# Attention and mixture of experts on one core: rank products in fp32r, a third turn of 64 columns, and the router's weights turned first

## The reference

```python
x = L0_attn_x
xn = _layernorm(x, axis=-1)
# attention: y = xn @ U (32 columns); softmax(-|y_i - y_j|^2) over the block's tokens, times xn
# feed-forward on xn (2048 tokens):
logits = rms_norm(xf) @ router_w.T                    # 8 experts
topk_p, topk_i = jax.lax.top_k(softmax(logits), 2)
order = jnp.argsort(~sel, axis=1, stable=True)        # sel: which tokens chose expert e
dispatch = order[:, :capacity]                        # capacity 320: the first 320 of them
xg = xf[dispatch]
eout = einsum(silu(xg @ rg) * (xg @ ru), rd)          # per expert: 128 -> 512 -> 128
routed = zeros.at[dispatch].add(eout * weight)
shared = silu(xn @ sg) * (xn @ su) @ sd               # 128 -> 1024 -> 128
return x + attention + shared + routed
```

## Time and profile before

| what | value |
|---|---|
| median of 3 runs | 158.22 us (157.16 to 158.99) |
| span of the profiled execution | 156.0 us |
| what lies outside the span, by the fastest, the median and the slowest run | 1.16, 2.22 and 2.99 us |
| PE busy | 151.1 us (97%) |
| DVE, ACT, POOL busy | 117.5, 103.8, 83.3 us |

### The profile page before, as it was taken

The page is one execution under the profiler, slowest core; times in us unless marked ns, Lnnn a source line. Parts: engine busy times, 40 slices in busy tenths (PEclk is TensorE's granted clock), DMA queues, the critical chain, the costliest instruction groups (busy, mean ns, idle before and its releaser), DMA issues.

```text
span 156.0 us, 3115 instructions
## 1 busy us (share of the span) xinstructions
PE 151.1 (97%) x964; PEld 135.6 (87%) x964; DVE 117.5 (75%) x290; ACT 103.8 (67%) x217; POOL 83.3 (53%) x102
## 2 busy tenths in 40 slices
PE   6899999999999999999999999999999999999992
PEld 6878878798999988888878999999999999878992
DVE  3799969899824599999997676786787786545962
ACT  3258999999479398768756669899686566343200
POOL 7562531357777778878400004698988857454000
PEclk9999999999999999999999999999999999999999
DMA  4999999992111117536059400314232111118477
GB/s 118 278 274 119 147 277 335 345 335 77 57 53 51 51 32 220 158 80 191 0 119 299 136 0 2 149 39 119 60 105 70 32 46 34 29 29 263 100 267 217
DMA packets 26640, 20.72 MB, mean 133 GB/s; under 512 B 2334, under 2 KB 22841, under 8 KB 26625
## 3 DMA queue, kind: packets, MB, share of 16 engines
q1 hardware_dynamic: 24832, 17.89, 44.3%
q0 software_dynamic: 1792, 2.65, 5.6%
HBM read 12.36 MB, written 7.92 MB: 130 GB/s over the span
## 4 chain that ended last, share of the span: by engine, by line
PE 92%; DMA 2%; ACT 2%; DVE 2%; POOL 1%; issue 1%; SPq 0%
PE bank L1257 9%; PE bank L1342 9%; PE bank L1177 8%; PE bank L1179 8%; PE bank L1178 8%; PE bank L1282 8%; PE bank L1288 8%; PE bank L1285 8%; PE bank L1398 5%; PE bank L1400 5%; PE bank L1399 5%; PE bank L1414 2%; PE bank L1242 2%; DMA acc<-in_L_attn_x_dram 2%; PE bank L1425 2%; PE bank L1197 1%
## 5 line engine op out<-in xcount | busy, mean ns | idle before, releaser
L676 ACT ACTIVATE silu<-bank 128x512 f32<-128x512 f32 (+1 forms) x64 | 33.3, 520 | 29.3 <-PE bank L1288 29.1
L570 POOL DMA_INDIRECT slots_dram<-row,slot_i x32 | 34.0, 1063 | 10.9 <-issue 9.4
L1008 DVE TENSOR_TENSOR bank<-bank,silu 128x320 f32<-128x320 f32 (+1 forms) x48 | 27.1, 565 | 15.6 <-ACT silu L676 12.6
L589 POOL DMA_INDIRECT routed_dram<-eo,xg x24 | 23.0, 957 | 11.5 <-DVE eo L1048 6.3
L1014 DVE TENSOR_TENSOR hid_lo<-bank,hid_hi 128x320 fp32r<-128x320 f32 (+1 forms) x48 | 26.2, 546 | 0.0
L684 ACT CAST hid_hi<-bank 128x320 fp32r<-128x320 f32 (+1 forms) x48 | 22.9, 477 | 0.0
L577 POOL TENSOR_TENSOR ew_lo<-sw_raw,ew_hi 128x1024 fp32r<-128x1024 f32 x3 | 7.2, 2416 | 19.4 <-ACT ew_hi L700 19.4
L1342 PEld LDWEIGHTS bank<-sd,hid_s 128*128 128x128 f32 x128 | 14.8, 192 | 0.3
L1008 DVE TENSOR_TENSOR hid_s<-bank,silu 128x512 f32<-128x512 f32 x16 | 11.0, 685 | 5.5 <-PE bank L1179 5.2
L1257 PEld LDWEIGHTS bank<-row,probs 128*128 128x128 f32 x128 | 14.8, 192 | 0.2
L1342 PE MATMUL bank<-sd,hid_s 128*128 128x128 f32 x128 | 15.0, 275 | 0.0
(11 more groups left out here) (204 smaller groups left out, 363.8 us busy)
## 6 DMA issues: line engine op xcount, KB each, us to landing
sw_raw<-in_L_ffn_rg_dram SPq DMA_DIRECT2D x8, 256.0 KB, 3.0
sw_raw<-in_L_ffn_ru_dram SPq DMA_DIRECT2D x8, 256.0 KB, 3.5
rd_raw<-in_L_ffn_rd_dram SPq DMA_DIRECT2D x8, 256.0 KB, 3.4
routed_dram<-fill SPq DMA_DIRECT2D x1, 2048.0 KB, 12.6
routed<-routed_dram SPq DMA_DIRECT2D x8, 256.0 KB, 4.0
slots_dram<-fill SPq DMA_DIRECT2D x1, 1300.0 KB, 12.6
xg<-slots_dram SPq DMA_DIRECT2D x8, 130.0 KB, 2.4
row<-row SPq DMA_DIRECT2D x1, 1024.0 KB, 8.2
```

The lines of the kernel that those rows point to most:

```text
L570: G.indirect_dma_start(slots_dram, bass.IndirectOffsetOnAxis(slot_i[:, k, t:t + 1], 0), row[:, t, 0:RW], None, bounds_check=E * CAP - 1, o ...
L676: C.activation(silu[:, q % 2, 0:n], gate_bank(q)[:, 0:n], ACT.Silu).then_inc(silu_ready, 1)
L1008: V.tensor_tensor(hid, up[:, 0:n], silu[:, q % 2, 0:n], ALU.mult).then_inc(hid_ready, 1)
```

## The change

Three edits, and what they bring with them:

1. `sel`, `slot0` and `tri` become fp32r. `slot0` has all 128 rows (each 1/128 of the start) in place of one, `sel` lies by expert and not by token, and the products take `ones_r` and `tri` (rounded copies that ACT makes ahead of everything else, once `consts` says that POOL has set their sources).
2. The third turn of an expert's sums takes the 64 columns that hold something, so its output has 64 partitions. By the rule above that instruction takes 128 x 64 of the array.
3. The router's weights are loaded by ACT's own DMA queue, as ACT's first instruction, and no longer by SP's; and TensorE turns them ahead of `turn(0)`.

```diff
-        tri = sb("tri", [P, P], BF16)
+        tri_f = sb("tri_f", [P, P])
+        tri = sb("tri", [P, P], F32R)
...
+        ones_r = sb("ones_r", [P, P], F32R)
...
-        slot0 = sb("slot0", [P, E, NT], BF16)
+        slot0 = sb("slot0", [P, E, NT], F32R)
...
-        sel = sb("sel", [P, NT, E], BF16)
+        sel = sb("sel", [P, E, NT], F32R)
...
-            sp.dma_start(rw_raw[:, :], rw_in).then_inc(rw_loaded, 16)
...
+            act.dma_start(rw_raw[:, :], rw_in).then_inc(rw_loaded, 16)
+            act.wait_ge(consts, 1)
+            C.copy(tri[:, :], tri_f[:, :])
+            C.copy(ones_r[:, :], ones_f[:, :]).then_inc(rank_consts, 1)
             root_of(PASSES[0])
...
-            V.tensor_copy(slot0[:, :, :], slot0_i[:, :, :]).then_inc(slot0_set, 1)
+            V.tensor_scalar(slot0[:, :, :], slot0_i[:, :, :], 1.0 / P, None, ALU.mult).then_inc(slot0_set, 1)
...
-                V.tensor_tensor(sel[:, :, :], chosen[:, 0, :, :], chosen[:, 1, :, :], ALU.add
-                                ).then_inc(sel_ready, 1)
+                V.tensor_tensor(sel[:, :, :].rearrange("p e t -> p t e"), chosen[:, 0, :, :], chosen[:, 1, :, :],
+                                ALU.add).then_inc(sel_ready, 1)
...
                 pe.wait_ge(slot0_set, 1)
-                s = sel[:, :, :].rearrange("p t e -> p e t")
-                M(rank_ps, tri[:, :], s, start=True, stop=False)
-                M(rank_ps, ones_bf[0:1, :], slot0[0:1, :, :], start=False, stop=True)
-                M(tot_ps.rearrange("p (e t) -> p e t", e=E), ones_bf[:, :], s, start=True, stop=True).then_inc(rank_done, 1)
+                pe.wait_ge(rank_consts, 1)
+                M(rank_ps, ones_r[:, :], slot0[:, :, :], start=True, stop=False)
+                M(rank_ps, tri[:, :], sel[:, :, :], start=False, stop=True)
+                M(tot_ps.rearrange("p (e t) -> p e t", e=E), ones_r[:, :], sel[:, :, :], start=True, stop=True
+                  ).then_inc(rank_done, 1)
...
-                for i in range(TG if JOBS[job][0] == "block" else 3):
-                    last = nc.tensor.transpose(turn_b[1][:, P * i:P * i + P],
-                                               turned_out[:, P * i:P * i + P], ident[:, :])
+                n = width(closing_chunk(JOBS[job]))
+                for i in range(0, n, P):
+                    m = min(P, n - i)
+                    last = nc.tensor.transpose(turn_b[1][0:m, i:i + P], turned_out[:, i:i + m], ident[:, :])
...
             pe.wait_ge(consts, 1)
+            pe.wait_ge(rw_loaded, 16)
+            nc.tensor.transpose(rw_ps, rw_raw[:, :], ident[0:E, 0:E]).then_inc(rw_turned, 1)
             turn(0)
             warm(10)
             first_chunk()
-            pe.wait_ge(rw_loaded, 16)
-            nc.tensor.transpose(rw_ps, rw_raw[:, :], ident[0:E, 0:E]).then_inc(rw_turned, 1)
```

More of the change, by code:

```diff
@@ L311, in moe_attention_kernel @@
         fill_set, fill_zeroed = sem("fill_set"), sem("fill_zeroed")
+        rank_consts = sem("rank_consts")
         ones_set, slot0_set = sem("ones_set"), sem("slot0_set")
@@ L489, in _ @@
                             fill=0.0, base=0, pattern=[[-1, P]], channel_multiplier=1).then_inc(ident_set, 1)
-            G.affine_select(out=tri[:, :], in_=minus_ones[:, :], compare_op=ALU.is_ge,
+            G.affine_select(out=tri_f[:, :], in_=minus_ones[:, :], compare_op=ALU.is_ge,
                             fill=0.0, base=0, pattern=[[-1, P]], channel_multiplier=1)
```

## The result

| what | before | after |
|---|---|---|
| median (least to most), 21 runs each | 157.47 us (156.79 to 159.22) | 158.16 us (158.09 to 159.25) |
| ratio, 95% interval | | 1.0045 (1.0028 to 1.0061) |

The changed kernel is 0.7 us slower, where 160.7 had been forecast. The three runs shown before the prediction had a median of 158.22; 21 runs have 157.47. The profiled execution of after is its longest run: 159.25 us with a span of 157.5. At the root, `turn(0)`, the ranks, the scores and the attention the two agree within 0.02 us; the small turn, which has room there, stands at 6.98 in the one and at 7.33 in the other.

What follows compares the result with a forecast made beforehand. PE was taken to bound the kernel, with no slack in the experts' stretch (80.4 to 133.1 us). 158.22 + 2.4 + 0.16 - 0.1 + 0 = 160.7 us, range 158.6 to 161.8.

Steps and rivals of the forecast that it cites:

- the price of the third turn: PE, experts' stage: the 64-column turn's weight load isn't run ahead; 8 x 0.30 = 2.4 us slower.
- no price: Rival: the third turn's load runs ahead; each turn costs 0 to -0.056 us, kernel 157.8 to 158.3; chance 0.20.
- The second rival: Third turn in half the columns takes two passes, 0.11 us more each, 161.6 us in all; chance 0.10.
- ACT's start: Casts and a table load ahead of ACT's first root move it from 5.56 to 5.72: +0.16 us, bounds 0 and 0.3.
- The router's turn: PE wins 0.34 us at 10.8 us, little of which arrives: -0.1 us, bounds 0 and -0.34.
- The rank products: PE's three rank products gain 0.48 us at most, but later work waits for DVE anyway: 0.
- The base: Starting time of the sum: median run 158.22 us, profiled span 156.0, with 2.22 us outside it untouched.

Runs made afterwards that it cites:

- e6: Kernel before with one more turn of the router's weights (32 x 128 of the array) ahead of each expert's three turns; ratio 1.0202.
- e9: Kernel before with one more plain fp32 product (128 x 32, at column 96) ahead of each expert's three turns; ratio 1.0224.
- e1: Kernel before with only the third turn cut to 64 columns; 157.44 us, ratio 1.0003.
- e7: Kernel before with one more turn of 32 columns (128 x 32 of the array) ahead of each expert's three turns; ratio 1.0102.
- e11: Kernel before with a plain fp32 product of 16 columns (128 x 32, at column 0) ahead of each expert's turns; 160.87 us, one run.
- e2: Kernel before with two casts of 128 columns, read by nothing, ahead of ACT's first root; 158.06 us, ratio 1.0046.
- r2: Changed kernel profiled once more, no edit; 158.15 us, span 156.4.
- e5: Kernel before with only the router's weights loaded by ACT's queue and turned ahead of `turn(0)`; 157.55 us, ratio 0.9992.
- e4: Changed kernel with the wait and both casts moved behind ACT's copy of the router's weights; 157.6 us, ratio 0.9985.
- e3: Changed kernel with a square root of a constant ahead of the casts, so the root's table loads first; 157.99 us, ratio 1.0024.
- e12: Kernel before with a plain fp32 product of 128 columns (128 x 128) ahead of each expert's turns; 160.09 us, one run.

## Why the prediction was wrong

**The step that failed: the price of the third turn.** "So a load for another part of the array isn't run ahead, neither on the way in nor on the way out" was read from a turn in part of the rows and from the norms, a plain two-pass product in part of the columns. Both readings hold where they were made: moved into the experts' stage, the first costs 0.30 us in the chain (e6; 0.34 at 10.8 us), and the second 0.25 (e9). They were carried to an instruction that shares only half of each: a turn, as the one, in part of the columns, as the other. The term of 2.4 us measured 0.05 (-0.27 to 0.35; e1). The text had the doubt in its rival "no price", which gave 157.8 to 158.3, and weighed it down by "that one load was late by the same 0.07 as the row changes". Of the Trainium skill's sentence cited there ("TensorE: Matmul & The Clock Gate", Part 2, step 1), by which a load is pulled ahead if the row groups don't conflict or if it goes to the background buffer, the condition on rows fits the turns of e1, e6 and e7. It doesn't explain e9 to e11, whose rows did not change and whose loads were late; which loads go to the background buffer no run shows. The rival's gain of up to 0.45 us is not there either: the shorter load lay under a matmul already.

**The second rival,** two passes, fell as well: one matmul of 272 ns for each turn. What the Trainium skill has in "TensorEngine Tiling (Array Packing)", Restrictions, that column tiling disables the transpose mode of fp32, was not borne out by the eight turns of 128 x 64, nor by e7's.

**ACT's start: right in mechanism, mis-sized.** The root was forecast at 5.72 and stands at 5.71. The term of 0.16 (bounds 0 to 0.3) measured 0.7: 0.46% of 157.41 in e2 (0.25 to 0.67%, 0.4 to 1.05 us). It was counted from the root at 5.56 of one execution, taken as a property of the kernel, where DVE's wait of 0.91 us for the second half of x ran ahead of it. The eleven other executions without casts ahead of the root have it at 4.65 to 5.21. Against the first profile the term was right: 0.15 at the root, 0.07 at the attention. What was not looked at is whether the point that the new wait replaced was itself the accident of a DMA. How the roots of all 21 runs lie isn't in the profiles.

**The router's turn: right as far as the traces go.** Its chunks lost the break at 10.8, and -0.1 was forecast to arrive. After and r2, with the turn moved, reach the attention 0.08 to 0.09 us ahead of e2, which has the same start without it. Part of the 0.34 us that PE wins goes into its wait for DVE's `xnT_lo`, 0.5 us in after and r2 and 0.3 in e2; the text had looked to ACT's cast, by an overlap of 0.1 us between its operations that is 0.01 in the earlier trace rows. As a time it lies inside e5's interval, so no run shows it. What the turn is worth behind an early root stays open: e4 is ahead of all others at the attention, and e5 is not.

**The rank products: 0, right.** They won 0.23 us, and all of it goes into the wait for `yL` ahead of the scores. The text had said that PE would wait elsewhere, without naming this wait. No run has this edit alone.

**The base.** 158.22 was the median of three runs, 0.75 above that of 21. The profiled executions that have a time as well as a span (after, and those of the experiments) put 1.69 to 1.80 us outside it, not the 2.22 of the sum, so the profiled 156.0 belonged, by this estimate, to a run of 157.7 to 157.8. The sum with what was measured: 157.47 + 0 + 0.7 + 0 + 0 = 158.2, against 158.16; the 0.7 is taken from e2 and not worked out ahead. That the time fell into the range of the "no price" rival is in part chance: its +0.06 and its base were both off, in opposite ways.

## What to carry to other kernels

A price read at one instruction holds for its kind: before it is carried over eight times, list what differs (rows or columns, turn or product, one pass or two), and give the reading that shares least the lesser weight. Where an edit puts work ahead of an instruction that waits for a DMA, count its cost from the earliest that the DMA lands, not from where the instruction stood in one execution. Casts put first on ScalarE took a table load of their own, and the root's, which had hidden under the first DMA, came into the path: they belong behind its first use.

## What was not expected of the hardware

Beside the array's parts: POOL's issue of an indirect DMA took 0.97 us in most places, but 1.43 to 1.49 in some. In e3's timelines of POOL and of DVE, the four from 60.32 to 65.65 begin 0.03 to 0.09 us behind the start of a DVE subtraction between two operands in SBUF. Two of the four:

```profile
59.05 0.97 POOL L573 DMA_INDIRECT slots_dram<-row,slot_i  x1 [0.30 <-issue]
60.32 1.43 POOL L573 DMA_INDIRECT slots_dram<-row,slot_i  x1 [0.30 <-issue]
62.06 1.49 POOL L573 DMA_INDIRECT slots_dram<-row,slot_i  x1 [0.30 <-issue]
```

```profile
60.23 0.68 DVE L1029 TENSOR_TENSOR ew_lo<-sw_raw,ew_hi 128x512 fp32r<-128x512 f32 x1
...
62.02 0.68 DVE L1029 TENSOR_TENSOR ew_lo<-sw_raw,ew_hi 128x512 fp32r<-128x512 f32 x1
```

e3 has five issues over 1.4 us; before, e4 and r2 have four, and after has three. e12 has five too, and it is the only other profile in which PE waits for the first expert's scattered rows by as much, 0.6 us. So e3's wait of 0.5 us fits one or two more such issues of 0.5 us, and would be where part of its earlier start went. That is argued, not shown: no run changed this alone.
